# Second attention's row spill ahead of its deals, and six projected value tiles instead of ten

## The reference, cut to what matters

```python
# layer 0: 16 heads, 4 key/value heads, q and k of width 128 with rotary embedding, v of width 16
v = (x @ wv).reshape(B, S, N_KV_HEAD, DV)          # 512 x 256 @ 256 x 64
band = (j <= i) & (j > i - 64)                      # a query sees the last 64 keys
front_ok = (j < 32) & (j <= i - 64)                 # and the first 32
out = softmax(q @ k.T / sqrt(128) + mask) @ v

# layer 1: 16 heads of width 16, no mask; b, s = 4, 512
Q, K, V = X @ Wq + bq, X @ Wk + bk, X @ Wv + bv
out = softmax(q @ k.T / sqrt(16)) @ v
out = out.transpose(0, 3, 2, 1).reshape(b, s, 256) @ Wo + bo     # for each sequence features, then tokens, then heads
```

## Time and profile before

| | |
|---|---|
| median of 3 runs | 1076.05 us (1074.58 to 1078.24) |
| profiled execution | 1076.98 us |
| its span, first to last instruction | 1075.1 us |
| mean granted TensorE clock | 0.931 |
| busy: TensorE, VectorE, ScalarE, GpSimd | 929.8, 667.7, 492.8, 281.2 us |
| the second attention's first score (line 979) in batches 0 to 3 starts at | 236.97, 483.29, 729.89, 976.53 us |

### The profile page before, as it was taken

The page is one execution under the profiler, slowest core; times in us unless marked ns, Lnnn a source line. Parts: engine busy times, 40 slices in busy tenths (PEclk is TensorE's granted clock), DMA queues, the critical chain, the costliest instruction groups (busy, mean ns, idle before and its releaser), DMA issues.

```text
span 1075.1 us, 14422 instructions
## 1 busy us (share of the span) xinstructions
PE 929.8 (86%) x5184; PEld 571.6 (53%) x5184; DVE 667.7 (62%) x1656; ACT 492.8 (46%) x983; POOL 281.2 (26%) x216
## 2 busy tenths in 40 slices
PE   4646888799888999989888999979887999979986
PEld 1434556645325677745334667845333767845433
DVE  4987567638646567538746567546746666655753
ACT  4454565042463765131663665231554666222443
POOL 0655465000002676000001577100000658100000
PEclk9868799989898999989988999989899999989988
DMA  6210001154001110046001110027000100018000
GB/s 218 84 34 10 16 20 40 45 147 109 2 2 44 36 50 11 1 105 151 2 2 44 31 50 16 1 64 192 2 2 30 40 25 2 1 44 211 2 2 20
DMA packets 45751, 51.24 MB, mean 48 GB/s; under 512 B 6000, under 2 KB 35440, under 8 KB 45680
## 3 DMA queue, kind: packets, MB, share of 16 engines
q1 hardware_dynamic: 42976, 47.47, 16.2%
q10 hardware_dynamic: 2384, 1.79, 0.5%
q0 software_dynamic: 320, 1.05, 0.3%
HBM read 37.44 MB, written 12.58 MB: 47 GB/s over the span
## 4 chain that ended last, share of the span: by engine, by line
PE 65%; DVE 19%; ACT 7%; issue 4%; DMA 3%; SPq 2%; POOL 1%; ACTq 0%; DVEq 0%; POOLq 0%
PE bank L784 12%; PE bank L826 6%; PE bank L1025 6%; DVE mx L1362 5%; PE bank L979 5%; PE bank L901 5%; PE bank L885 5%; PE bank L873 5%; PE bank L1010 4%; PE bank L1037 3%; PE bank L967 2%; DVE w1T L1112 2%; PE bank L864 2%; PE bank L838 2%; PE bank L1015 2%
## 5 line engine op out<-in xcount | busy, mean ns | idle before, releaser
L514 POOL TENSOR_TENSOR region<-region 128x512 f32<-128x512 f32 x80 | 109.6, 1369 | 495.6 <-DVE region L1207 490.9
L1362 DVE TENSOR_REDUCE mx<-bank 128x1 f32<-128x512 f32 x256 | 166.7, 684 | 94.2 <-PE bank L979 93.4
L738 ACT ACTIVATE region<-bank 128x512 f32<-128x512 f32 x256 | 132.7, 604 | 74.4 <-PE bank L1015 74.1
L784 PE MATMUL bank<-xnT,wrope 128*128 128x512 f32 x320 | 148.9, 609 | 9.6 <-ACT xnT L618 9.6
L651 ACT ACTIVATE region<-region,nb 128x224 f32<-128x224 f32 (+1 forms) x256 | 97.6, 451 | 108.7 <-DVE nb L1216 108.4
L826 PE MATMUL bank<-V,region 128*128 128x224 f32 x384 | 91.2, 384 | 28.3 <-DVE nb L1216 21.9
L979 PE MATMUL bank<-Kp,Qp 64*128 64x512 f32 x256 | 93.5, 485 | 21.2 <-DVE mx L1362 15.7
L510 POOL TENSOR_TENSOR region<-region,sin_sb 128x512 f32<-128x512 f32 x60 | 78.4, 1307 | 85.5 <-ACT region L631 85.5
L784 PEld LDWEIGHTS bank<-xnT,wrope 128*128 128x128 f32 x320 | 61.8, 197 | 71.0 <-issue 60.2
L826 PEld LDWEIGHTS bank<-V,region 128*128 128x128 f32 x384 | 73.5, 201 | 40.6 <-DVE nb L1216 24.1
L1201 DVE TENSOR_TENSOR region<-bank,cos_sb 128x512 f32<-128x512 f32 x80 | 54.3, 689 | 49.3 <-PE bank L784 49.1
(11 more groups left out here) (130 smaller groups left out, 1495.5 us busy)
## 6 DMA issues: line engine op xcount, KB each, us to landing
wrope<-in_wrope SPq DMA_DIRECT2D x80, 128.0 KB, 2.1
scratch<-region SPq DMA_DIRECT2D x32, 256.0 KB, 3.6
Qp<-scratch SPq DMA_DIRECT2D x64, 128.0 KB, 3.5
Kp<-scratch SPq DMA_DIRECT2D x64, 128.0 KB, 3.6
X<-in_x SPq DMA_DIRECT2D x4, 512.0 KB, 4.2
scratch<-region SPq DMA_DIRECT2D x16, 128.0 KB, 3.6
out<-X SPq DMA_DIRECT2D x16, 128.0 KB, 1.7
wpT<-in_wgu SPq DMA_DIRECT2D x3, 512.0 KB, 11.2
```

What stands on the lines that cost most here:

```text
L514: nc.gpsimd.tensor_tensor(dst, dst, sw[:, r % 2, :], ALU.add)\
L738: nc.scalar.activation(P1[:, n % 8, :], t_ring[n % 4][:, :], ACT.Exp, scale=SCALE1)\
L784: mm = nc.tensor.matmul(misc(name)[:, 0:width], lhs(c), xnT[:, c, :], start=(c == 0), stop=(c == DC - 1))
L1362: nc.vector.tensor_reduce(mx1[:, g % 2, column:column + 1], s_bank[i % 2][:, :], AX.X, ALU.max)\
```

## The change

On SyncE both halves are now spilled before any group is dealt. On TensorE the values are projected at six places: tiles 0 to 3, the last 64 tokens (tile 4 of the bank), and the front keys in rows 64 to 95 of tile 5. VectorE makes three copies: tiles 0 to 3; rows 0 to 63 of bank tiles 2, 3, 4 to `V0` tiles 4, 5, 6 (the first 64 rows of the next tile are the window's end); and the front, read three times over, to rows 64 to 95 of `V0` tiles 4 to 6. The count that `attend0` and the bank's release wait for goes from 2 to 3.

```diff
-        v0_ready = sig("v0_ready", 2)
+        v0_ready = sig("v0_ready", 3)
...
-                "v0": lambda: [(v0_ready, 2)],
+                "v0": lambda: [(v0_ready, 3)],
...
                 for half in range(2):
                     spill(b, half)
-                    deal(b, 2 * half)
-                    deal(b, 2 * half + 1)
+                for g in range(NG):
+                    deal(b, g)
...
-                places = [(0, P, 0, 0)]
-                for t in range(1, TT):
-                    places += [(t, P, 0, t * P - WIN), (TT - 1 + t, WIN, 0, t * P + WIN),
-                               (TT - 1 + t, FRONT, WIN, 0)]
+                places = [(0, P, 0, 0)] + [(t, P, 0, t * P - WIN) for t in range(1, TT)]
+                places += [(TT, WIN, 0, SEQ - WIN), (TT + 1, FRONT, WIN, 0)]
...
-                    pe.wait_ge(v0_ready.sem, v0_ready.at(b, 2))
+                    pe.wait_ge(v0_ready.sem, v0_ready.at(b, 3))
...
-                src = misc(("v0",))[:, 0:(2 * TT - 1) * NKV * DV]\
+                src = misc(("v0",))[:, 0:(TT + 2) * NKV * DV]\
                     .rearrange("p (t g d) -> p t g d", g=NKV, d=DV)
                 nc.vector.tensor_copy(V0[:, 0:TT, :, 0:DV], src[:, 0:TT]).then_inc(v0_ready.sem, 1)
-                m = UNIT_W - P
-                nc.vector.tensor_copy(V0[0:m, TT:, :, 0:DV], src[0:m, TT:]).then_inc(v0_ready.sem, 1)
+                nc.vector.tensor_copy(V0[0:WIN, TT:, :, 0:DV], src[0:WIN, 2:TT + 1]).then_inc(v0_ready.sem, 1)
+                front = src[WIN:WIN + FRONT, TT + 1:TT + 2].broadcast_to([FRONT, TT - 1, NKV, DV])
+                nc.vector.tensor_copy(V0[WIN:WIN + FRONT, TT:, :, 0:DV], front).then_inc(v0_ready.sem, 1)
```

## The result

The changed kernel takes 1095.88 us (median of 6 executions, 1090.31 to 1101.45) against 1077.99 us before in the same comparison: 1.0169 times as long, 95% interval 1.0141 to 1.0197, or 17.9 us more by the medians. It can differ by 0.1 to 0.2% from the quotient of the medians.) The forecast was slower, 1088.0 us with 1093.0 as its upper end; the direction was right, the size was not.

A forecast was written before the change was run, and what follows sets the result against it. TensorE was taken as the main bound (65% of the chain), with SyncE and DMA setting the second attention's start. Values 0, queue 7.9, backlog 1.2 and clock 2.8 made 11.9 us over 1076.05: 1088.0 us, range 1080.5 to 1093.0.

The forecast's parts named there:

- Values, forecast 0: Projection early in each batch: 1.73 us less TensorE work hidden behind GpSimd's last rotation; cost 0, bounds -0.1 to +0.35 per batch.
- Place and sign of the loss: SyncE's queue before the first deal: six added issues replace a shorter landing wait, delaying the first score; 7.9 us in sum.
- The backlog: Deals find the second spill in the DMA engines and take longer: 0.3 us per batch (0 to 1.0), 1.2 us.
- Nothing takes it up again: After the first score: everything hangs on it score by score, so the delay is not recovered.
- The clock: TensorE after the longer stall: clock falls to the low level, 1.4 us each, two falls, 2.8 us; bounds 0 and 6.
- The queue's part: Delay of the first deals plus backlog: 9.1 us, low end 2.8 us, high end 13 us.
- The high ends: Upper bounds: 13 us for issues and backlog, up to 6 for the clock, 1.4 for the copies.
- Rival (e): Deals' packets wait for the whole second spill: 1 us per batch, three or four falls, 1093 to 1095; chance 0.08.

The follow-up runs named there:

- e2_spill_order_only: Kernel before with only the new queue order (both spills ahead of all deals), values as before: 1091.74 us, ratio 1.0150.
- e4_fill_stall: Full change plus 14 unused TensorE matmuls while it waits for the first deal: 1088.41 us, ratio 1.0126 to the kernel before.
- e7_after_up8: Full change with all eight FFN chunks ahead of the first score instead of six: 1096.52 us, ratio 1.0177 to the kernel before.
- e1_values_only: Kernel before with only the values part (six places projected), old queue order: 1076.98 us against 1077.07, ratio 1.0006.
- e3_group0_first: Against the kernel before: first spill, deal of group 0, second spill, then deals of groups 1 to 3: 1074.42 us, ratio 0.9987.
- e8_before_up8: Kernel before with all eight FFN chunks ahead of the first score: 1088.78 us, ratio 1.0098.
- e9_before_fill_norm: Kernel before with 20 unused TensorE matmuls in the wait for each batch's second normalisation: 1071.51 us against 1078.28, ratio 0.9938.
- e5_six_small: Kernel before plus six 8 KB writes on SyncE's queue between first spill and the wait for its landing: 1088.06 us, ratio 1.0094.
- e6_pool_spill: Second spill's six writes issued on GpSimd's queue, SyncE keeping first spill, wait, deals: 1092.71 us, ratio 1.0136 to the kernel before.
- e11_three_ahead: Against the kernel before: three of the second spill's six writes inside the first landing wait, three behind group 0's deal: 1081.06 us, ratio 1.0025.
- e10_best: Six-place values, group 0 dealt before the second spill, 20 plus 12 unused matmuls in two TensorE waits: 1070.51 us, ratio 0.9941 to the kernel before.

## Why the prediction was right and wrong

**Values, forecast 0.** Right: a ratio of 1.0006, inside noise, and the cover was the one named, the last rotation. The copies were as priced, within 0.01 us (0.34 and 0.36 us against 0.30 to 0.35).

**Place and sign of the loss.** Right: six issues take the place of a wait that was shorter than they are, SyncE's queue hands it to the first deal, and the score starts that much later. The first deal came 3.0, 2.8, 1.3 and 3.3 us later after the first write than before, where I had 2.5, 2.5, 1.3 and 2.45: 10.4 us against 8.75. From the end of the first spill's issues to the first deal it was 5.0 to 5.2 us in three batches and 5.6 in batch 3 instead of 4.97, and in batches 0 and 3 the first spill's own issues took 0.3 us more than before.

**The backlog: the step that failed most.** I took 0.3 us per batch, with 1.0 as the end. The distance from first deal to first score grew from 6.80, 6.86, 6.65 to 7.68, 7.65, 7.86, and in batch 3 from an assumed 6.8 to 7.52: 3.6 us in all instead of 1.2. The term also looked in the wrong place. It priced a later landing of the deals, and that came out as forecast: from the eighth issue to the score the four batches need 1.0 us more together. But I let the deals themselves be issued at the pace of before, and there 2.6 us were added: the first deal took 1.10, 0.76, 1.14 and 0.67 us instead of 0.35, and the eighth was issued 3.92, 3.71, 3.97 and 3.70 us behind the first instead of 3.2. The same span is 3.7 to 4.0 us in all 16 batches of the four profiles with this order (the change, `e2_spill_order_only`, `e4_fill_stall`, `e7_after_up8`), and 3.2 in the 20 of those with the old one or with only group 0 dealt first (the kernel before, `e1_values_only`, `e3_group0_first`, `e8_before_up8`, `e9_before_fill_norm`). `e5_six_small` has 1.0 of the 2.6 us with next to no data; the rest goes with the second spill's data, which `e6_pool_spill` and `e11_three_ahead` show as a cost of its own. But in two batches of `e10_best` a single deal took 1.22 and 1.71 us to issue with no second spill in flight, so the data is not the only thing that can do it, and why an issue takes longer stays open. The waits sum to 13.1 us where I had 9.1.

**Nothing takes it up again.** Right: in batch 3, where the clock held, the stretch from first score to main loop took 24.56 us, and 24.57 before, though it began behind a stall of 3.12 us.

**The clock.** The mechanism was right: 1.5 us per fall against 1.4. There were three falls in the profiled execution, I had taken two: 4.5 against 2.8 us. `e4_fill_stall` removes just these. I had no term for the main loops (2.3 us), where the clock wanders from execution to execution.

In sum: 1.6 us by which the first deals were later than forecast, 2.4 between first deal and first score, 1.7 behind the stalls (a third fall, for the most part) and 2.3 in the main loops went beyond the forecast, 0.4 elsewhere came back: 7.6 us. The queue's part, 13.1 us, came out at the high end of its own bounds (13), the falls inside theirs (4.5 of 0 to 6). The high ends together give 1096.5, which would have held the result; the stated end of 1093.0 was set well below them. Rival (e), heavy backlog with three or four falls, was the one that came, with 0.9 us of backlog per batch (it names 1) and three falls. The Trainium skill's sentence that the time to start a DMA is usually small beside the DMA ("DMA: Bandwidth & Descriptors", Issuing engines are not separate DMA queues) does not hold here: in `e5_six_small` six writes of 8 KB took 4.31 us to issue, 0.72 each, beside a median of 1.9 us from issue to landing. What the Trainium skill says in the same section, that transfers share the same 16 engines whichever queue they come from, fits `e6_pool_spill`, where writes issued by GpSimd took the distance of SyncE's deals to the score from 6.86 to 9.35 us.

## What to carry to other kernels

Ahead of a transfer that somebody waits for, a queue should carry nothing that is not needed yet: an unneeded write costs its issue time and its data, and filling the wait for a landing with it gained nothing here, since its result has no waiter. Look for the first consumer of each transfer (here eight deals of thirty-two) and order by that. A cut in an engine's work is worth what the last arrival at the next join says, and a stall on TensorE costs itself and, where the clock falls behind it, what that loses (1.5 us each time here).

## What the runs showed that I had not expected

Moving TensorE's work ahead of a start that waits for DMA brought nothing, although the stall went from 14.45 to 2.3 us. Unused matmuls in a wait made the old kernel 0.6% faster. Stalls of 2.3 to 2.8 us ahead of the first score were sometimes followed by the low clock and sometimes not: in `e5_six_small` 2.27 and 2.40 us were, in `e2_spill_order_only` 2.67, 2.52 and 2.73 us were not. So one profiled execution says little about how often the clock falls.
